# A fused conditioned residual chain: one transpose, one product and three split jobs moved in hand-written engine orders

## What is computed

```python
# x is (64, 32, 512); it_lora, it_cond, it_lang hold one index for each of the 64 batches
def l0(x):                      # gated MLP, 512 -> 1376 -> 512, with a rank-16 adapter for each batch
    gate = x @ W_gate.T + 0.5 * (x @ A_gate[it_lora].T) @ B_gate[it_lora].T
    up   = x @ W_up.T   + 0.5 * (x @ A_up[it_lora].T)   @ B_up[it_lora].T
    act  = silu(gate) * up
    return act @ W_down.T + 0.5 * (act @ A_down[it_lora].T) @ B_down[it_lora].T
x = x + l0(x)
x = x + einsum('bct,bcd->bdt', x, W1[it_cond])      # mixes the 32 channels of a batch
x = x + (x @ W.T + 2 * sum_of_top2_experts(x))      # top 2 of 8 experts, rank 16, language bias
x = x + einsum('bct,bcd->bdt', x, W3[it_cond])
```

## Time and profile before

| | us |
|---|---|
| three runs | 584.95, 585.10, 585.92 |
| median | 585.1 |
| the profiled execution | 585.92, its span 584.0 |
| TensorE busy within the span | 569.5 (98%) |
| VectorE busy | 304.4 (52%) |
| ScalarE busy | 204.0 (35%) |
| GpSimd busy | 223.9 (38%) |
| mean granted TensorE clock | 0.997 of full |

### The profile page before, as it was taken

How to read it: one execution, slowest core, us unless ns; L and a number is a source line. 1 busy time by engine, 2 the same in 40 slices (tenths; PEclk the granted TensorE clock), 3 DMA queues, 4 the chain that set the end, 5 groups by cost and what they waited for, 6 DMA issues and landing times.

```text
span 584.0 us, 8799 instructions
## 1 busy us (share of the span) xinstructions
PE 569.5 (98%) x3371; PEld 514.2 (88%) x3371; DVE 304.4 (52%) x697; ACT 204.0 (35%) x413; POOL 223.9 (38%) x227
## 2 busy tenths in 40 slices
PE   5989999999999999999999999999999999999996
PEld 5878988888989898989898989898989898999995
DVE  4886353535353434444444444434343657777776
ACT  4764242323333333333233232323232433333321
POOL 5442143656565646441313131413231302433421
PEclk9999999999999999999999999999999999999998
DMA  8991343343534343442424242424242911243322
GB/s 273 364 335 59 109 136 101 107 155 122 161 124 153 123 149 127 145 155 75 137 77 136 76 138 75 137 76 136 76 137 72 339 42 54 73 154 118 114 85 73
DMA packets 34889, 77.38 MB, mean 133 GB/s; under 512 B 5216, under 2 KB 9632, under 8 KB 34848
## 3 DMA queue, kind: packets, MB, share of 16 engines
q1 hardware_dynamic: 23952, 39.56, 20.2%
q0 software_dynamic: 10752, 37.23, 19.9%
q10 hardware_dynamic: 144, 0.03, 0.0%
HBM read 64.22 MB, written 12.58 MB: 132 GB/s over the span
## 4 chain that ended last, share of the span: by engine, by line
PE 91%; DMA 3%; DVE 2%; issue 1%; POOL 1%; ACT 1%; POOLq 0%; DVEq 0%; ACTq 0%
PE gu_ps L1148 13%; PE gu_ps L1150 13%; PE gu_ps L1149 13%; PE down_ps L1148 8%; PE down_ps L1149 8%; PE down_ps L1150 8%; PE l_ps L1148 5%; PE l_ps L1149 5%; PE l_ps L1150 5%; PE gu_ps L1155 3%; PE gu_ps L1156 3%; PE act_t L1218 3%; DMA b_sel_raw<-b_gu,idx_rank 1%; PE x2t_ps L1272 1%; DMA a_raw<-a_all,idx_batch 1%
## 5 line engine op out<-in xcount | busy, mean ns | idle before, releaser
L666 POOL DMA_INDIRECT b_sel_raw<-b_gu,idx_rank x48 | 47.7, 994 | 189.2 <-PE gu_ps L1156 176.3
L1148 PE MATMUL gu_ps<-w_sb,xt 128*128 128x512 f32 x256 | 104.7, 409 | 0.7 <-DVE w_sb L928 0.7
L1148 PE MATMUL down_ps<-wd_sb,act_hl 128*128 128x288 f32 (+1 forms) x352 | 105.1, 299 | 0.0
L1149 PE MATMUL down_ps<-wd_sb,act_hl 128*128 128x288 f32 (+1 forms) x352 | 103.8, 295 | 0.0
L1150 PE MATMUL down_ps<-wd_sb,act_hl 128*128 128x288 f32 (+1 forms) x352 | 103.6, 294 | 0.0
L1150 PE MATMUL gu_ps<-w_sb,xt 128*128 128x512 f32 x256 | 100.6, 393 | 0.0
L1149 PE MATMUL gu_ps<-w_sb,xt 128*128 128x512 f32 x256 | 100.2, 391 | 0.0
L666 POOL DMA_INDIRECT a_raw<-a_all,idx_batch x64 | 76.6, 1198 | 57.9 <-DVE wd_sb L928 38.1
L782 ACT CAST act_hl<-act_t 128x256 fp32r<-128x256 f32 (+1 forms) x64 | 27.3, 452 | 135.1 <-PE act_t L1218 135.1
L773 ACT ACTIVATE act<-gu_ps 128x512 f32<-128x512 f32 (+1 forms) x47 | 26.1, 555 | 126.5 <-PE gu_ps L1156 126.5
L928 DVE TENSOR_TENSOR act_hl<-act_t,act_hl 128x256 fp32r<-128x256 f32 (+1 forms) x64 | 32.0, 520 | 71.8 <-ACT act_hl L782 71.8
(11 more groups left out here) (147 smaller groups left out, 1114.6 us busy)
## 6 DMA issues: line engine op xcount, KB each, us to landing
w_sb_raw<-wgu SPq DMA_DIRECT2D x16, 256.0 KB, 9.9
x_res<-x_rows SPq DMA_DIRECT2D x16, 256.0 KB, 2.9
x_after_l<-x_res SPq DMA_DIRECT2D x16, 256.0 KB, 2.3
bd<-bd_hl SPq DMA_DIRECT2D x16, 256.0 KB, 2.0
x<-x_after_l SPq DMA_DIRECT2D x16, 256.0 KB, 2.7
bd_hl<-bd SPq DMA_DIRECT2D x16, 256.0 KB, 4.6
xt_raw<-x_t SPq DMA_DIRECT2D x15, 256.0 KB, 2.5
out<-y SPq DMA_DIRECT2D x15, 256.0 KB, 2.0
```

The source lines that it names most:

```text
L666: nc.gpsimd.indirect_dma_start(out=dst, out_offset=None, in_=table, in_offset=bass.IndirectOffsetOnAxis(ap=idx, axis=0)).then_inc(s, 16)
L1148: pe.matmul(out_, stationary[0], moving[0], start=start, stop=False, skip_group_check=True)
L1149: pe.matmul(out_, stationary[0], moving[1], start=False, stop=False, skip_group_check=True)
```

## The change

Three moves. TensorE: `transpose_t(1)` goes from behind `transpose_act(0)` into the middle of `gate(3)`, after its first two pieces; and `down(0)` goes from behind `gate(4)` to ahead of it, right behind `adapters(3)`. ScalarE and VectorE: of the jobs of step 2, `("b", 3)` goes from second place to behind `wd_items(0)`, and `("act", 0)` goes from last place to ahead of it; `("gate", 2)` is then last. No instruction is added or taken away, and SyncE's and GpSimd's lists stay as they are.

```diff
--- before.py
+++ after.py
@@ -215,7 +215,7 @@
         return {-1: first_items() + [("at", 0)],
                 0: wgu_items(1, 0) + [("tm", 0), ("b", 0), ("t", 0)] + wgu_items(1, 1) + [("b", 1), ("gate", 0)],
                 1: [("at", 1)] + wgu_items(2, 0) + [("gate", 1), ("tm", 1), ("adt", 0), w2u[0], ("t", 1)] + w2u[1:],
-                2: [("b", 2), ("b", 3), ("adt", 1)] + wd_items(0) + [("gate", 2), ("act", 0)],
+                2: [("b", 2), ("adt", 1)] + wd_items(0) + [("act", 0), ("b", 3), ("gate", 2)],
                 3: [("gate", 3)] + wd_items(1) + [("act", 1), ("b", 4)],
                 4: [("gate", 4), ("bd", 0)] + wd_items(2) + [("act", 2), ("b", 5), ("x", 2, 0)],
                 5: [("tdm", 0), ("td", 0), ("act", 3), ("x1", 0), ("at", 2), ("gate", 5), ("b", 6)],
@@ -1335,14 +1335,15 @@
             whole(up, 1)
             adapters(1)
             x_a(1)
-            whole(gate, 3)
+            gate(3, 0, HC // 2)
+            transpose_t(1)
+            gate(3, HC // 2, HC)
             transpose_act(0)
-            transpose_t(1)
             whole(up, 3)
             adapters(2)
             adapters(3)
+            down(0)
             whole(gate, 4)
-            down(0)
             transpose_act(1)
             whole(up, 4)
             adapters(4)
```

## The result

| | median, us | runs, us |
|---|---|---|
| before, beside the changed kernel | 585.41 | 584.95 to 585.92 |
| changed kernel | 589.34 | 588.71 to 590.17 |

The ratio is 1.0069, 95% interval 1.0054 to 1.0085: slower, as forecast, but outside the range of 586.0 to 588.2. It lies on the rival in which the clock falls in the new wait, 589.3 us.

A forecast was written before the change was run, and what follows sets the result against it. TensorE, busy 569.5 of 584.0 us, bounds the kernel, taking turns with VectorE between 30 and 39 us. 1.84 later at adapters(3) less 0.08 at down(0) gives 1.76, taken as 1.8: 585.1 + 1.8 = 586.9 us, range 586.0 to 588.2.

The forecast's parts named there:

- the rival in which the clock falls in the new wait: Behind the wait ahead of adapters(3), half clock costs 2.4 us more, giving 589.3 us; chance 0.1.
- VectorE's chain: VectorE's jobs from ("b", 2) at 33.4 us to ("b", 3) at 37.45, through at 38.68 us.
- The step that decided: adapters(3) waits for ("b", 3), now behind more VectorE work, and starts at 38.73 us, 1.84 us later.
- `down(0)` covered: down(0) ahead of gate(4) has its waits covered, by 0.6 us for ("gate", 2), and gains 0.08 us.
- the delay carried to the end by a dense TensorE: Behind gate(4), 1.76 us late, TensorE is dense and nothing gives the delay back.
- the upper of the two bounds: VectorE's weight pieces ahead of ("act", 0) take 1.81 or 1.92 us.
- the bounds that the sum had: ("t", 1) 0.36 or 0.52 us, weight pieces 1.81 or 1.92, landing 0 or 0.15: total 1.65 to 2.1 us.
- The transpose: transpose_t(1) within gate(3): a new TensorE wait of about 0.6 us, and about 0.6 us gained at adapters(2).
- the base: Median of the three runs of the kernel before, 585.1 us, to which 1.8 us was added.

The follow-up runs named there:

- The filled wait: Changed kernel with 28 small matmuls that nothing reads put between adapters(2) and adapters(3): 587.80 us, ratio 1.0036 to the kernel before.

## Why the prediction was wrong: VectorE's chain right, the clock left out

**The direction and the chain were right, the time was not.** The step that decided, `("b", 3)` behind seven of VectorE's instructions, came as told: no idle on VectorE, `adapters(3)` at 38.72 us, `down(0)` covered, and the delay carried to the end by a dense TensorE. Its size was a little short. From mask to `adapters(3)` the changed kernel takes 38.72 - 29.09 = 9.63 us and the kernel before 36.89 - 29.32 = 7.57: + 2.06 where I had 1.84. The profiled execution had merely begun 0.23 us early. The missing 0.2 are three starts: `t_hl` 0.71 us behind `w2u[0]` instead of 0.60, the weights behind it 0.46 instead of 0.40, and `("act", 0)` 1.92 us behind the start of the weight pieces, the upper of the two bounds. The first of the three lay outside the bounds that the sum had; and the lower end of that sum, given as 1.65 us, comes to 1.70 from its own terms. The filled wait (587.80, + 2.2 us) and the one execution at full clock (587.73) measure this term by itself. With it alone the time would have lain in the range of 586.0 to 588.2.

**The transpose was right:** 0.5 us of new wait, 0.5 us gained at `adapters(2)` counted from the mask (34.43 - 29.09 = 5.34 us against 35.18 - 29.32 = 5.86), where 0.6 was forecast for each, and none of it at the end, since the gather bounds `adapters(3)` at its old place.

**The step that failed is the price of TensorE's matmuls behind the new wait.** The sum took `adapters(3)`, `down(0)` and `gate(4)` at their length before, at full clock; what the clock could cost stood at nothing in it and outside the range, in a rival with a chance of 0.1. The runs showed 0.50 of the clock for 5.7 us behind the wait, and a cost of 2.66 us in the profiled execution and 1.7 us in the medians (+ 3.9 on before with the wait open, + 2.2 with it filled). The rival's mechanism came true. That its 589.3 us is also the measured median is in part luck: its price of 2.4 us was 0.7 too high against the medians, and the chain, at 1.8, was 0.4 too low and the base, 585.1 against 585.4, 0.3. I gave it 0.1 because "no row shows a fall after a wait". That was an argument from rows not looked for. The kernel before has the fall in its own last 6 us, a granted clock of 0.53 over the nine matmuls of the last burst, behind waits of under 1 us each; the last digit of the clock line on its page is an 8 among 9s. And the start, where TensorE comes out of an idle of 6.3 us at half pace, is a case of half pace behind idle too, though one in which TensorE had not worked before. With two cases of half pace behind idle or sparse work, and no idle of 3 us without it, this rival deserved more than the forecast that left it out. The Trainium skill, "TensorE: Matmul & The Clock Gate", section "Why this matters for your kernels", asks for short gaps for just this reason; here the trace agrees, with 3.5 us of idle and 0.50 of the clock behind it, and all but one of the 22 executions have the time and the mean clock of such a fall.

**What stays open.** What decides whether an idle of 2.6 us brings the fall. By time and mean clock it came in 3 of 4 executions of one kernel, and, as a second idle behind one of 1.4 us, in all four of another (clocks 0.994 and 0.996). Nor is it shown what sets the length of the slow stretch, some 3 to 6 us in four traces. It may be why the changed kernel's executions scatter over 2 us, but only one of them has a trace: the eleven with a mean clock of 0.993 or 0.994 average 589.9 us and the ten with 0.996 or 0.997 589.3, and the longest of all, 590.74, has 0.997.

## What to carry to other kernels

A wait that a reordering lengthens has two prices: its length, and what the clock loses behind it. In these runs the second price came behind single waits of 2.6 and 3.5 us and not behind one of 1.4. Before one accepts a wait of that length on a dense TensorE, one should look for work that can stand in it; moving one independent product there turned a loss of 3.9 us into a gain of 0.8. When one lane of splits feeds TensorE, the lane's order should be the order of TensorE's needs, worked out for both together: neither half of this change alone was faster than the two, and TensorE's moves alone put a second wait, of 2.6 us, into the kernel.

## What the runs showed of the hardware that was not expected

- Judged by time and mean clock, the half clock came behind idles of 3.5 us nearly always (21 of 22 executions of the changed kernel), behind a single one of 2.6 us in 3 of 4, behind 1.4 us in none of ten. In the last burst of the kernel before it stood behind waits of 0.7 and 0.8 us with 1.0 us of matmuls between; the changed kernel has the same two waits there, and full clock behind them. The slow stretch lasted 5.8 us in one trace and 2.9 to 3.5 us in three.
- The fall isn't always seen in the wait. Over the wait of 3.5 us the granted clock reads 0.87 in one trace and 0.94 in another; in a third it is 1.00 over both idles and 0.53 from the first matmul behind them.
- At the start of the launch the granted clock reads 1.00 while the matmuls stand at half pace; there the distance of their starts tells the clock, and the granted clock doesn't.
- Filling a wait with small matmuls that nothing reads kept the clock at 1.00 in the profiled execution and cost nothing that shows: 1.7 us less for the changed kernel (each against the kernel before), 0.0 for the one before.
